# Row scores of two heads in two neighbouring PSUM banks, with one maximum for both

## The reference

```python
# x: 32 x 100 x 256, ctx: 32 x 361 x 256
z  = layernorm(x)                                  # the queries' side
q, k, v = z @ Wq.T + bq, ctx @ Wk.T + bk, ctx @ Wv.T + bv     # 16 heads of 16
attn = softmax(einsum('bhqd,bhkd->bhqk', q, k))    # 100 x 361 a head, no scaling
x = x + layernorm(attn @ v + z) * gamma + beta
# then x + FFN(layernorm(x)): layernorm, router over 8 experts, top 2, gelu MLP 256-512-256
```

## Time and profile before

| | |
|---|---|
| median of 3 runs | 909.34 us (908.41 to 911.66) |
| profiled execution, its own time | 911.36 us |
| its span, first to last instruction | 909.6 us |
| mean granted TensorE clock | 0.925 |
| busy over the span: PE, DVE, ACT, POOL | 782.1, 678.1, 510.6, 547.7 us |
| L949 (maxima) | 512 operations, 251.4 us busy, 523 ns each |
| L620 (row scores) | 512 matmuls, 134.3 us busy |

### The profile page before, as it was taken

The page is one execution under the profiler, slowest core; times in us unless marked ns, Lnnn a source line. Parts: engine busy times, 40 slices in busy tenths (PEclk is TensorE's granted clock), DMA queues, the critical chain, the costliest instruction groups (busy, mean ns, idle before and its releaser), DMA issues. The chain is left out here.

```text
span 909.6 us, 26604 instructions
## 1 busy us (share of the span) xinstructions
PE 782.1 (86%) x8118; PEld 611.0 (67%) x8119; DVE 678.1 (75%) x1883; ACT 510.6 (56%) x1351; POOL 547.7 (60%) x609
## 2 busy tenths in 40 slices
PE   3659799999999999999999986519599999999970
PEld 2436577777777777777776653319599888888960
DVE  5379799999999999999998886755655565565640
ACT  2336478888888888888887654410243333333420
POOL 4223577777777777868776553430257667667750
PEclk9989799999999999999999988755599999999995
DMA  5764457676666757576768764354033343333427
GB/s 147 159 167 107 92 127 164 145 164 141 158 150 148 162 131 166 139 168 137 163 142 195 186 139 124 102 139 147 24 59 57 61 69 59 60 62 63 72 39 144
DMA packets 155679, 110.93 MB, mean 122 GB/s; under 512 B 68274, under 2 KB 149570, under 8 KB 155106
## 3 DMA queue, kind: packets, MB, share of 16 engines
q1 hardware_dynamic: 134004, 80.37, 38.6%
q0 software_dynamic: 11360, 17.37, 11.5%
q10 hardware_dynamic: 10270, 12.62, 4.7%
HBM read 39.99 MB, written 23.88 MB: 70 GB/s over the span
## 5 line engine op out<-in xcount | busy, mean ns | idle before, releaser
L949 DVE TENSOR_REDUCE negmax<-s_row 100x1 f32<-100x361 f32 x512 | 251.4, 523 | 30.0 <-PE s_row L620 22.9
L783 ACT ACTIVATE p_t<-s_t 128x400 f32<-128x400 f32 x384 | 188.9, 502 | 67.0 <-PE s_t L639 65.7
L620 PE MATMUL s_row<-k_stack,q_stack 125*128 125x361 bf16 x512 | 134.3, 326 | 21.8 <-DVE negmax L949 10.0
L639 PE MATMUL s_t<-q_stack,k_stack 128*128 128x100 bf16 x1536 | 129.0, 211 | 13.9 <-DMA q_stack<-m_part 9.0
L639 PEld LDWEIGHTS s_t<-q_stack,k_stack 128*128 128x128 bf16 x1536 | 93.3, 99 | 61.9 <-issue 27.4
L1216 PE MATMUL p_h<-zgt,w_k 128*128 128x128 f32 x912 | 115.6, 280 | 3.2 <-DVE w_k L1403 3.2
L1262 ACT ACTIVATE hidt<-p_h,b_k 128x128 f32<-128x128 f32 x228 | 65.2, 368 | 89.1 <-PE p_h L1216 89.1
L1216 PEld LDWEIGHTS p_h<-zgt,w_k 128*128 128x128 f32 x912 | 107.5, 193 | 8.9 <-issue 7.3
L1225 PE MATMUL p_y<-k_stack,hidt 128*128 x456 | 107.7, 379 | 0.0
L606 PE MATMUL pj<-wv_s,ct 128*128 128x256 f32 x384 | 106.8, 401 | 0.5 <-ACT k_rest L749 0.5
L575 PE MATMUL pj<-ct,wk_s 128*128 128x361 f32 x256 | 96.1, 500 | 10.0 <-DMA bk_s<-in_bk 8.9
(11 more groups left out here) (180 smaller groups left out, 1381.4 us busy)
## 6 DMA issues: line engine op xcount, KB each, us to landing
k_stack<-k_part SPq DMA_DIRECT2D x192, 192.0 KB, 3.6
q_stack<-q_part SPq DMA_DIRECT2D x186, 64.0 KB, 2.0
ct<-in_ctx_t SPq DMA_DIRECT2D x32, 361.0 KB, 4.7
w_s<-in_w ACTq DMA_DIRECT2D x8, 512.0 KB, 4.4
k_stack<-in_w ACTq DMA_DIRECT2D x8, 512.0 KB, 5.3
zscr<-zn SPq DMA_DIRECT2D x32, 100.0 KB
z_in<-zscr SPq DMA_DIRECT2D x32, 100.0 KB
zf_d<-zf_s SPq DMA_DIRECT2D x32, 100.0 KB
```

The lines of the kernel that those rows point to most:

```text
L620: nc.tensor.matmul(s_row[h % 2][:, 0:KEYS], q_stack[0:MROW, b.slot, h, :], k_stack[0:MROW, b.slot, h, 0:KEYS], start=True, stop=True).then ...
L639: last = nc.tensor.matmul(s_t[g % 2][:, j * Q:j * Q + Q], k_stack[:, b.slot, h, kt * 128:kt * 128 + 128], q_stack[:, b.slot, h, 0:Q], star ...
L783: nc.scalar.activation(p_t[:, quad % 2, kt, :], s_t[g % 2][:, 0:4 * Q], ACT.Exp).then_inc(exp_done, 1)
L949: v.tensor_reduce(negmax[:, b.slot, h:h + 1], s_row[h % 2][0:Q, 0:KEYS], AXIS.X, ALU.max, negate=True).then_inc(max_done, 1)
```

## The change

The two banks become one tensor of two neighbouring banks, `s_rows`. `row_max` becomes `rows_max`: one VectorE operation reads both heads' scores and writes both columns of `negmax`. It waits for both matmuls. `max_done` now counts pairs, so TensorE waits for it once per pair, for the whole operation before, and then writes both banks; ScalarE's wait for all maxima of a batch is counted in pairs too. The aggregate of the layer norm, which stood between the two maxima, now stands behind the one operation.

```diff
-            s_row = [pb(att, f"s_row{k}", [128, 512]) for k in range(2)]
+            s_rows = pb(att, "s_row", [128, 2, 512])
+            s_row = [s_rows[:, k] for k in range(2)]
...
-                    after(pe, max_done, H * b.index + h - 1)
+                    if h % 2 == 0:
+                        after(pe, max_done, H // 2 * b.index + h // 2)
                     nc.tensor.matmul(s_row[h % 2][:, 0:KEYS], q_stack[0:MROW, b.slot, h, :],
                                      k_stack[0:MROW, b.slot, h, 0:KEYS], start=True, stop=True).then_inc(s_row_done, 1)
...
-                            act.wait_ge(max_done, H * b.index + H)
+                            act.wait_ge(max_done, H // 2 * b.index + H // 2)
...
-                def row_max(b, h):
-                    dve.wait_ge(s_row_done, H * b.index + h + 1)
+                def rows_max(b, h):
+                    dve.wait_ge(s_row_done, H * b.index + h + 2)
                     if h == 0:
                         after(dve, m_split, M_STEPS * (b.index - 3) + 2)
-                    v.tensor_reduce(negmax[:, b.slot, h:h + 1], s_row[h % 2][0:Q, 0:KEYS], AXIS.X, ALU.max, negate=True).then_inc(max_done, 1)
+                    v.tensor_reduce(negmax[:, b.slot, h:h + 2], s_rows[0:Q, :, 0:KEYS], AXIS.X, ALU.max, negate=True).then_inc(max_done, 1)
...
-                        for h in heads_now[:1]:
-                            row_max(b, h)
+                        for h in heads_now[::2]:
+                            rows_max(b, h)
                         for e in firsts:
                             aggregate(e, 0)
                         for e in seconds:
                             aggregate(e, 1)
-                        for h in heads_now[1:]:
-                            row_max(b, h)
                         for e in firsts:
                             variance(e, 0)
```

## The result

The changed kernel takes 932.05 us (median of 4 runs, 930.16 to 933.75), before 909.12 in the runs beside it: ratio 1.0235, interval 1.0212 to 1.0258 (the two medians by themselves give 1.025). It is 2.3% slower. The forecast was 930.5 us, range 908 to 950. The profiled execution took 931.37 us, its span is 929.6, 20.0 more than before.

A forecast was written before the change was run, and what follows sets the result against it. TensorE was taken to set the time in most of a period, VectorE for a stretch at pairs 7 and 8. Losses of 18.2, 2.1 and 0.9 us gave +21.2, hence 930.5 us, range 908 to 950.

The forecast's parts named there:

- The cost of the operation: On VectorE: one maximum over two banks takes 914 ns, saving 0.06 us a pair against two back to back.
- The new waits: At each pair: maxima start 0.15 us later, after both matmuls; TensorE waits for the whole operation before.
- The aggregate's part: Behind the maxima: variance starts 0.20 us after the aggregate, 0.07 us later than the maxima's own delay.
- The holds: TensorE's waits for the merged maximum before pairs 7 and 8, some 0.4 to 0.5 us each.
- 26 regular periods x 0.70: Regular part of the attention loop: every period loses 0.70 us, 18.2 us in all.
- the walk: One period's eight pairs of row scores retimed: TensorE late by 0.07 us at pair 4, 0.70 after pair 8.
- The three periods before them ... 2.1 us: Three attention periods ahead of the regular ones: same pairs, 0.7 us lost in each.
- Three of them at 0.3 give 0.9: Last periods of the loop: VectorE late less often, so three periods lose 0.3 us each.
- A: Attention loop: VectorE is the bound and the larger operation pays; -14 us, 895 us; chance 0.07.
- B: Attention loop: the losses are absorbed, less than 0.15 us a period left; 909 us; chance 0.10.
- C: Operation takes 1.05 us, every hand-over 0.14: about 1.6 us a period, 956 us; 0.13 for more than 945.
- D: Attention loop: the halted TensorE loses its clock, about 1.5 us more a period; +65 us, 975 us; chance 0.03.

The follow-up runs named there:

- e5: The kernel before with one operation for two maxima in pairs 1 to 4 only, pairs 5 to 8 as before; 913.20 us, ratio 1.0031.
- e6: The kernel before with one operation for two maxima in pairs 5 to 8 only, pairs 1 to 4 as before; 931.34 us, ratio 1.0209.
- e2: The kernel before, but TensorE waits for both maxima of a pair before writing the next; VectorE starts at the first matmul; 928.17 us.
- e3: The kernel before, but a pair's first maximum waits for both matmuls; TensorE still waits bank by bank; 921.40 us, ratio 1.0122.
- e4: The changed kernel with the layer norm's aggregate moved ahead of the maxima, into VectorE's wait for the pair; 923.84 us, ratio 1.0136.
- e1: The kernel before, still two maxima a pair, but both wait for both matmuls and TensorE for both maxima; 935.38 us, ratio 1.0265.
- e7: The kernel before with the aggregate and its memset moved ahead of the first maximum; 910.27 us, ratio 1.0001.

## Why the prediction was right

**What bounds the kernel.** That the hand-over in pairs costs time where VectorE is late, at pairs 5 to 8, and next to none elsewhere is shown by e5 and e6: +0.05 and +0.71 us a period.

**The cost of the operation.** Forecast 914 ns (at least 895), measured 905. Two maxima back to back are busy only 0.97 us, since they overlap, so the saving in time is 0.06 to 0.07 us a pair, and not the 0.14 by which 905 ns is less than two durations. The Trainium skill (Perfetto Trace Analysis, Optimizing Scalar/DVE Operations) puts VectorE's overhead at about 125 ns an instruction on PSUM, as time of the busy engine and not as the duration that a profile shows. By it the large operation would take an estimated 0.97 - 0.125 = 0.85 us; the measured saving is half of the page's figure.

**The new waits.** Both were named, and e2 and e3 show both: +0.44 and +0.36 us a period. The aggregate's part, 0.20 us between it and the variance, is measured at 0.20 (317.26 to 317.46) and shown by e4. The holds were forecast at 0.4 to 0.5 us and are 0.38 and 0.54. That banks should rotate so that one's evacuation overlaps the next group's matmuls (the Trainium skill, Perfetto Trace Analysis, Matmuls) has the sign right here: e1, which gives up only that, costs 2.65%.

**The sum.** The total is right, 20.0 us of span for 21.2, but its terms aren't, and that they make up for each other is luck.

"26 regular periods x 0.70": the walk itself holds. The part from pair 5 to pair 8 was forecast at 0.63 (0.70 less the 0.07 of pair 4) and is 0.64, and the hold at pair 4 came, 0.05. But one period stood for all. In the kind of period that was walked 0.08 of it is regained ahead of pair 5: from pair 4 to pair 5 it is 1.71 us after (314.21 to 315.92) and was 1.79. In the next kind that step was 1.70 before, nothing is regained, and the loss is 0.70 as forecast. In the third kind, where the loop turns over, the kernel before spends 5.17 or 5.30 us from pair 8 to the next pair 1 (5.70 the first time), and 4.96 or 4.98 in the others, of which 0.2 is the wait inside pair 8. The changed kernel spends 4.76 in every kind (4.89 the first time). The rows of the values' matmuls behind pair 8 show it, first before at the loop's turn, then before in a plain period, then after at the loop's turn:

```profile
300.11 0.69 PEld L651 LDWEIGHTS zt<-p_t,v_aug 128*32 128x32 f32 x24 [0.23 <-issue]
300.11 0.91 PE L651 MATMUL zt<-p_t,v_aug 128*32 128x100 f32 x24
...
315.88 0.73 PE L651 MATMUL zt<-p_t,v_aug 128*32 128x100 f32 x24
...
307.51 0.72 PE L653 MATMUL zt<-p_t,v_aug 128*32 128x100 f32 x24
```

Here the prediction had said that TensorE is busy through. The extra time is there each of the seven times that the code goes back to the start of the loop, and not when the loop is left behind batch 27 (4.96), so it belongs to the turn; the profile names no wait for it, and why the changed kernel is nearly free of it (e1 is not, with 5.01 us for 4.76) was not tried. So 24 periods lost 13.9 us, 0.58 each.

"The three periods before them ... 2.1 us": 0.4 us. "Three of them at 0.3 give 0.9" for the last periods: of the 5.0 us between batches 27 and 31, the first two periods have 0.7 each, as regular ones, and the last two 1.6 and 2.0. I had argued that VectorE is late less often there. It is late for longer, as the timeline of the changed kernel shows at pairs 4 to 7 of the last batch but one:

```profile
548.67 0.78 PE L622 MATMUL s_row<-k_stack,q_stack 125*128 125x361 bf16 x2
549.24 0.54 PE L641 MATMUL s_t<-q_stack,k_stack 128*128 128x100 bf16 x4
550.45 0.79 PE L622 MATMUL s_row<-k_stack,q_stack 125*128 125x361 bf16 x2 [0.67 <-DVE negmax L951]
...
555.07 0.78 PE L622 MATMUL s_row<-k_stack,q_stack 125*128 125x361 bf16 x2 [0.67 <-DVE negmax L951]
```

In the regular part the key projection (L576, 1.38 us) stands between pairs 4 and 5; for the last batches there are no keys left to project, so the pairs stand close together and the hand-over holds TensorE at pair 5 too, 0.67 us, in the kernel before 0.21. That the missing projection is the reason is read from the timelines, and no run tried it. A part of the 5.0 us goes with the clock: over these four periods the granted clock was 0.85, before 0.91, and TensorE was busy 66.0 us for 64.1 with the same work. e1 and e6, with 0.92 there, took 75.7 and 74.8 us for the four, a loss of 3.2 and 2.2.

**The rivals.** A (VectorE's saved time counts) is out by e5. B (absorbed) has a little truth, 0.12 us a period in the mean. C did not come. D did not come in the regular part, where the clock stayed at 1.00 with two holds of 0.4 to 0.5 us a period; in the last four periods the clock did fall, by 0.06, but e7, which takes the time of the kernel before, has 0.88 there where that has 0.91, so that one execution of each can't say how much of it the change causes.

## What to carry to other kernels

Two banks that are handed over one at a time let the writer and the reader overlap; one larger operation over both turns them into a single buffer. Before merging, compare what the operation saves back to back (here 0.06 us) with what the pair's hand-over adds where the two engines run in close step (here 0.8 us a period). If such a change must be made, small operations that stood between the merged ones have to move ahead of them. Before an instruction is moved into a wait, see whether it fits: the guard of 0.78 us ended 0.2 us behind the pair. And walk one period of each kind, here three to a turn of the loop, and the last rounds of the pipeline, where the work that covered a wait is missing.

## What was not expected of the hardware

A loop of three periods doesn't make equal periods: at each of its turns TensorE lost 0.2 to 0.35 us in the kernel before (0.7 the first time), for which the profile names no wait, and next to nothing in the changed kernel.

At pair 5 of e6 the large operation starts 0.58 us behind the start of its pair, and 0.51 in the changed kernel, though both banks had long been free. e5 shows the same 0.07 us at pair 1 (0.66 to 0.69 for 0.60 to 0.62). e3, where TensorE waits for each bank as in e5 and e6, has 0.51 at pair 5 and 0.60 to 0.62 at pair 1. So it is neither the second wait alone nor the large operation alone, and the reason stays open.
